# A four-layer graph kernel: each direct transfer of 125 rows issued as one of 112 and one of 13 partitions

## What is computed

```python
x = _layernorm(x + attention(x, src, dst, edge_attr_8))      # layer 0
x = _layernorm(x + message(x, src, dst, edge_type_16))       # layer 1
x = _layernorm(x + equivariant(x, src, dst, edge_attr_4))    # layer 2
x = _layernorm(x + hypergraph(x, node=src, edge=dst))        # layer 3
# each layer: x[src] gathered, work per edge, segment_sum over dst (sorted);
# layer 3: node -> edge -> node -> batch norm -> node -> edge -> node, also over sorted src
```

## Time and profile before

| | us |
|---|---|
| median of three runs | 2641.88 |
| lowest, highest | 2640.07, 2645.51 |
| the profiled execution | 2639.84 |
| its span, first to last instruction | 2638.0 |

### The profile page before, as it was taken

One profiled execution on the slowest core, in us unless ns is written; L12 is line 12 of the kernel. 1 busy time (PEld: TensorE's weight loads), 2 busy tenths in 40 slices (PEclk: granted clock), 3 DMA queues, 4 the chain that ended last, 5 costly groups with the idle time before them and its releaser, 6 DMA issues. The chain is left out here.

```text
span 2638.0 us, 21630 instructions
## 1 busy us (share of the span) xinstructions
PE 1425.5 (54%) x4580; PEld 731.6 (28%) x4580; DVE 1606.3 (61%) x4851; ACT 863.9 (33%) x1813; POOL 1861.6 (71%) x1494
## 2 busy tenths in 40 slices
PE   6787588887266666546777456444554650011211
PEld 1443244444122222212333234222222330011110
DVE  8899387788258878938777544333334554434443
ACT  0111266677235566634665511111111320000000
POOL 5773878775388886254677687777874868878787
PEclk9899799999577777768898778777777875555555
DMA  1111344443435454343454467577696873333331
GB/s 25 28 33 40 95 118 121 125 112 81 96 75 126 124 129 128 93 102 88 109 127 115 89 169 194 158 168 192 180 157 184 226 202 94 86 67 70 74 72 43
DMA packets 350927, 297.90 MB, mean 113 GB/s; under 512 B 103741, under 2 KB 305228, under 8 KB 350781
## 3 DMA queue, kind: packets, MB, share of 16 engines
q1 hardware_dynamic: 253197, 225.40, 31.1%
q0 software_dynamic: 97600, 71.11, 14.3%
HBM read 199.75 MB, written 96.70 MB: 112 GB/s over the span
## 5 line engine op out<-in xcount | busy, mean ns | idle before, releaser
L2081 PE MATMUL tl_pX<-k_ident,tl_ga 125*128 125x125 f32 x400 | 84.2, 348 | 445.7 <-DMA tl_ga<-table_TE,k_s_idxE 332.0
L2192 DVE TENSOR_TENSOR_SCAN tl_S<-tl_same,tl_S,tl_pX 128x500 f32<-128x500 bf16 x96 | 120.3, 1254 | 315.9 <-PE tl_pX L2081 178.7
L471 POOL DMA_INDIRECT tl_ga<-table_TE,k_s_idxE x200 | 244.7, 1224 | 63.4 <-issue 59.4
L2081 PEld LDWEIGHTS tl_pX<-k_ident,tl_ga 125*128 125x128 f32 x400 | 57.3, 177 | 461.9 <-DMA tl_ga<-table_TE,k_s_idxE 342.1
L471 POOL DMA_INDIRECT eq_ga<-table_T,k_idxS x100 | 124.8, 1248 | 81.9 <-ACT eq_y L1786 52.9
L471 POOL DMA_INDIRECT ms_ga<-table_T,k_idxS x100 | 132.9, 1329 | 51.6 <-issue 42.0
L471 POOL DMA_INDIRECT tl_ga<-table_TH,k_send x100 | 122.7, 1227 | 58.7 <-issue 57.8
L1261 PE MATMUL tl_pCon<-dr_BC,dn_cT 128*128 128x512 f32 x196 | 135.0, 778 | 52.9 <-ACT dn_cT L1268 29.2
L471 POOL DMA_INDIRECT at_ga<-x,k_src x100 | 131.8, 1318 | 43.4 <-issue 25.2
L273 POOL DMA_INDIRECT table_ptab<-k_ef,ix_scatI x100 | 125.1, 1251 | 45.6 <-issue 45.6
L2032 POOL DMA_INDIRECT result<-tl_o,k_dst_end x100 | 121.8, 1218 | 44.3 <-issue 29.3
(11 more groups left out here) (464 smaller groups left out, 4455.0 us busy)
## 6 DMA issues: line engine op xcount, KB each, us to landing
dr_x<-x SPq DMA_DIRECT2D x97, 256.0 KB, 7.7
result<-dr_o SPq DMA_DIRECT2D x97, 256.0 KB, 5.1
dm_xT<-xT SPq DMA_DIRECT2D x32, 768.0 KB, 6.2
table_T<-at_y SPq DMA_DIRECT2D x50, 250.0 KB
table_T<-ms_y SPq DMA_DIRECT2D x50, 250.0 KB
table_T<-eq_y SPq DMA_DIRECT2D x50, 250.0 KB
table_TE<-tl_y SPq DMA_DIRECT2D x50, 250.0 KB
tl_fac<-table_dinv SPq DMA_DIRECT2D x50, 250.0 KB, 4.7
```

What stands on the lines that cost most here:

```text
L471: nc.gpsimd.indirect_dma_start(out=buf[:, k, :], out_offset=None, in_=table, in_offset=bass.IndirectOffsetOnAxis(ap=index[:, CT * c + k:CT ...
L2081: last = nc.tensor.transpose(pX[j % 2][:, k * TP:(k + 1) * TP], ga[j % RG][:, k, :], K["ident"][0:TP, 0:TP])
L2192: nc.vector.tensor_tensor_scan(S[i][:], same[j % RM][:], pX[i][:, 0:CE], 0.0 if j % NC == 0 else S[1 - i][:, CE - 1:CE], ALU.mult, ALU.add ...
```

## The change

`copy_rows` is new. It issues a transfer of 125 partitions as two, one of partitions 0 to 111 and one of 112 to 124, on the same queue one behind the other. All 300 transfers named above go through it (225 stores, 75 loads). Each part adds 16 to the semaphore, so every wait on these semaphores asks for twice the count. Rows, tables, buffers and order are the same. The diff, with the repeated places left out:

```diff
+SPLIT = 112
...
+def copy_rows(eng, out, given, sem):
+
+
+    for part in (slice(0, SPLIT), slice(SPLIT, TP)):
+        eng.dma_start(out[part], given[part]).then_inc(sem, 16)
...
-                sp.dma_start(rows_of(T["T1"], CE * c, CT), y[c % 2][:, 0:CT, :]).then_inc(s_st[c % 2], 16)
-                sp.dma_start(rows_of(T["T1"], CE * c + E, CT), y[c % 2][:, CT:2 * CT, :]).then_inc(s_st[c % 2], 16)
+                copy_rows(sp, rows_of(T["T1"], CE * c, CT), y[c % 2][:, 0:CT, :], s_st[c % 2])
+                copy_rows(sp, rows_of(T["T1"], CE * c + E, CT), y[c % 2][:, CT:2 * CT, :], s_st[c % 2])
...
-                sp.wait_ge(s_st[i], 32 * ((NC - i + 1) // 2))
+                sp.wait_ge(s_st[i], 64 * ((NC - i + 1) // 2))
...
-                sp.dma_start(xt[c % RX][:], rows_of(T["T1"], CE * c, CT)).then_inc(s_xt[c % RX], 16)
+                copy_rows(sp, xt[c % RX][:], rows_of(T["T1"], CE * c, CT), s_xt[c % RX])
...
-                sp.dma_start(z[c % RZ][:], rows_of(T["T2"], CE * c, CT)).then_inc(s_zd[c % RZ], 16)
+                copy_rows(sp, z[c % RZ][:], rows_of(T["T2"], CE * c, CT), s_zd[c % RZ])
...
         def stored(eng, n):
-            eng.wait_ge(s_st[0], 16 * ((n + 1) // 2))
-            eng.wait_ge(s_st[1], 16 * (n // 2))
+            eng.wait_ge(s_st[0], 32 * ((n + 1) // 2))
+            eng.wait_ge(s_st[1], 32 * (n // 2))
...
-                sp.dma_start(x[e % RL][:], rows_of(T["T3"], CE * e, CT)).then_inc(s_x[e % RL], 16)
+                copy_rows(sp, x[e % RL][:], rows_of(T["T3"], CE * e, CT), s_x[e % RL])
...
-                sp.dma_start(rows_of(T[TARGET[j // NC]], CE * (j % NC), CT), y[j % 2][:]).then_inc(s_st[j % 2], 16)
+                copy_rows(sp, rows_of(T[TARGET[j // NC]], CE * (j % NC), CT), y[j % 2][:], s_st[j % 2])
```

More of the change, by code:

```diff
@@ L743, in norm @@
                 act.wait_ge(s_r, c + 1)
-                need(act, s_st[c % 2], 32 * (c // 2))
+                need(act, s_st[c % 2], 64 * (c // 2))
                 for r in range(2 * CT):
@@ L1341, in load_targets @@
                 need(sp, s_h1, c - RX + 1)
-                sp.dma_start(xt[c % RX][:], rows_of(T["T1"], CE * c, CT)).then_inc(s_xt[c % RX], 16)
+                copy_rows(sp, xt[c % RX][:], rows_of(T["T1"], CE * c, CT), s_xt[c % RX])
             def store(c):
                 sp.wait_ge(s_y, c + 1)
-                sp.dma_start(rows_of(T["T2"], CE * c, CT), y[c % 2][:, 0:CT, :]).then_inc(s_st[c % 2], 16)
-                sp.dma_start(rows_of(T["T2"], CE * c + E, CT), y[c % 2][:, CT:2 * CT, :]).then_inc(s_st[c % 2], 16)
+                copy_rows(sp, rows_of(T["T2"], CE * c, CT), y[c % 2][:, 0:CT, :], s_st[c % 2])
+                copy_rows(sp, rows_of(T["T2"], CE * c + E, CT), y[c % 2][:, CT:2 * CT, :], s_st[c % 2])
             for s in range(-4, NC + 3):
@@ L1385, in biased @@
                 have(pool, c)
-                pool.wait_ge(s_xt[c % RX], 16 * (c // RX + 1))
+                pool.wait_ge(s_xt[c % RX], 32 * (c // RX + 1))
                 need(pool, s_h2, c - RU + 1)
@@ L1540, in residual @@
                 have(dve, c)
-                dve.wait_ge(s_xt[c % RX], 16 * (c // RX + 1))
+                dve.wait_ge(s_xt[c % RX], 32 * (c // RX + 1))
                 need(dve, s_n1, c - RU + 1)
@@ L1658, in load_targets @@
                 need(sp, s_y, c - RZ + 1)
-                sp.dma_start(z[c % RZ][:], rows_of(T["T2"], CE * c, CT)).then_inc(s_zd[c % RZ], 16)
+                copy_rows(sp, z[c % RZ][:], rows_of(T["T2"], CE * c, CT), s_zd[c % RZ])
             def store(c):
                 sp.wait_ge(s_y, c + 1)
-                sp.dma_start(rows_of(T["T3"], CE * c, CT), y[c % 2][:, 0:CT, :]).then_inc(s_st[c % 2], 16)
-                sp.dma_start(rows_of(T["T3"], CE * c + E, CT), y[c % 2][:, CT:2 * CT, :]).then_inc(s_st[c % 2], 16)
+                copy_rows(sp, rows_of(T["T3"], CE * c, CT), y[c % 2][:, 0:CT, :], s_st[c % 2])
+                copy_rows(sp, rows_of(T["T3"], CE * c + E, CT), y[c % 2][:, CT:2 * CT, :], s_st[c % 2])
             for s in range(-3, NC + 4):
@@ L1782, in norm @@
                 act.wait_ge(s_r, c + 1)
-                need(act, s_st[i], 32 * (c // 2))
+                need(act, s_st[i], 64 * (c // 2))
                 for r in range(2 * CT):
@@ L1839, in residual @@
                 b = c % RZ
-                dve.wait_ge(s_zd[b], 16 * (c // RZ + 1))
+                dve.wait_ge(s_zd[b], 32 * (c // RZ + 1))
                 have(dve, c)
@@ L2133, in out @@
                 act.wait_ge(s_psR, j + 1)
-                need(act, s_st[i], 16 * (j // 2))
+                need(act, s_st[i], 32 * (j // 2))
                 if phase == 1:
@@ L2208, in added @@
                 if e < NC:
-                    dve.wait_ge(s_x[i], 16 * (e // RL + 1))
+                    dve.wait_ge(s_x[i], 32 * (e // RL + 1))
                     nc.vector.tensor_tensor(z[i][:], x[i][:], bc(b2, CT), ALU.add).then_inc(s_z, 1)
```

## The result

The changed kernel takes 2615.08 us (median of four runs, 2614.43 to 2617.21), the kernel before 2640.98 in the same comparison: a ratio of 0.9903, 95% interval 0.9885 to 0.9921, or 25.9 us less. In a later comparison it was 2615.36 against 2641.81, 0.9900 (0.9884 to 0.9915). The profiled execution took 2617.21 us, its span 2615.3, which is 22.6 us less than the profiled one of before.

What follows compares the result with a forecast made beforehand. POOL's own issuing was taken to bound most of the kernel, so only its pauses could shrink: 4.8 + 1.0 + 18 + 10 = 33.8 us off 2639.84 gives 2606, adjusted to 2608 and rounded to 2610, range 2598 to 2634.

Steps and rivals of the forecast that it cites:

- Rival A: Whole kernel: shorter landings and vanishing stalls behind 125-partition transfers give 2610 us, own range 2600 to 2622; chance 0.55.
- the crowded stretch: Second pass, 1925 to 1967 us: VectorE's two waits, 23.5 us, blamed on whole `TH` stores; 16 us counted as gain.
- rival B: Only landings get shorter; gathers slow the second pass, VectorE's waits stay with another releaser; 2629 us, chance 0.22.
- the dense load's issue: Sign in the third pass: a dense load behind a store is issued in under 1 us instead of 3.2.
- the second pause: Sign in the tail, after the third pass: POOL's wait for the last dense store about 4 us instead of 14.09.
- the first pause: Sign in the tail, before the third pass: POOL's pause about 10 us instead of 28.57.
- the waits of under 5 us near 1940: Sign in the second pass: no dense load or `TH` store is waited for over 5 us there.
- Block ends: Ends of attention, message and equivariant: last split stores land sooner, 2.4 us each for two, 1.0 for the third.
- The 28.57 us pause: POOL before the third pass: 16 us from VectorE's waits and 2.4 from the last landing, together 18.
- The 14.09 us pause: POOL after the third pass: SP stalls behind 125-partition transfers go, so 10 us (2.4 to 13.8) is gained.
- Added issues: SP's 300 extra issues, some 0.4 us each, are covered by POOL's issuing; uncovered they would cost 120 us.
- Rival C: Parts use the same paths as the whole, nothing is spread: 2640 to 2645 us, chance 0.13.

## Why the prediction was right, and where it was not

The forecast was 2610, with 2598 to 2634, and the time is 2615. Rival A's own range holds it. Its mechanism for the third pass and the block ends is the one found. For the crowded stretch rival B was nearer. That the number came out this close is in part luck: the largest term was twice what it gave, and gains in message and equivariant that the sum did not have made up for a part. Of the signs named, the dense load's issue, the two block ends and about the second pause came; the first pause, and the waits of under 5 us near 1940, did not. POOL's mean for each gather moved in attention, from 1318 to 1384 ns, which the last section takes up. The steps one by one:

**Block ends, forecast 2.4 + 2.4 + 1.0.** From first store to next load 8.0 became 5.0, 8.1 became 5.0, and 11.1 became 11.6, which gives 3.0 + 3.1 - 0.5 = 5.6 against 5.8. The third ends with POOL's scatters, as the step said. The 3.0 of attention did not reach the time: the stretch is 429.3 in both. Among the other kernels it is 424.0 to 430.7 in no order of whole or split, 466.5 with the bad cut, so the noise of this stretch is as large as the term.

**Message and equivariant, forecast nothing beyond their ends.** This step was incomplete. Message takes 450.9 to 453.2 us in the three kernels with whole transfers there and 445.0 to 448.4 in the eight whose cut is at 100 or 112 or which have three parts, 5 us less and not 3. Equivariant is 370.7 to 374.2 against 365.9 to 367.9, with the end itself no shorter. The timeline of ScalarE in the kernel before shows one reason, which I had not looked at: at its end the next rows wait for a whole store to leave their buffer.

```profile
1487.99 1.65 ACT L1786 ACTIVATE eq_y<-eq_z,eq_nb,eq_rs 125x128 f32<-125x128 f32 x4 [1.94 <-DMA table_T<-eq_y]
...
1494.00 1.65 ACT L1786 ACTIVATE eq_y<-eq_z,eq_nb,eq_rs 125x128 f32<-125x128 f32 x4 [2.06 <-DMA table_T<-eq_y]
...
1501.47 1.65 ACT L1786 ACTIVATE eq_y<-eq_z,eq_nb,eq_rs 125x128 f32<-125x128 f32 x4 [4.09 <-DMA table_T<-eq_y]
```

After the change the same instructions wait 0.47 us for VectorE.

**The 28.57 us pause, forecast 18.** It gave 7.6, and the stretch 8.6. This is the step that failed: I put the two VectorE waits down to the whole `TH` store ahead of the dense loads and counted 16 of their 23.5 us as its doing. The waits are 12.73 and 13.28 us after the change, longer if anything. What I held against rival B, that only what stands behind a `TH` store pays the second half of the delay, was a reading of two places; both lie in the one stretch where four of five rows that the gathers read are one row. Spreading that row took the waits away with whole transfers too (none over 2.9 us, and a stretch of 466.2 us), so the gathers were the cause and the whole store at most an addition. Rival B had the right culprit and no reason for it: volume, my first thought, is out, and it is where the gathers read. Its sign, another releaser for VectorE's waits, did not come either, since both still end with a dense load: what a transfer waits behind is not named as its releaser. Rival B gave this term 2.4, so the measured 7.6 lies between the two.

**The 14.09 us pause, forecast 10.** It gave 8.6, to 5.51 us (6.13 in the second profile). The step held with its mechanism: the issue of a dense load fell from 3154 to 434 ns, and the whole load put back made the next issue 5.87 us again. What remains of lag and landing is 5.5 us where I had put 4, and the first was 14.09 in this profile but 17.25 and 17.41 in two other kernels with whole transfers there; with the tail all split and no other edit it is 5.51, 6.13 and 7.63.

**Added issues, forecast no cost.** Right. A third part, 300 issues more, shows none either.

**The sum.** The profiled time fell by 22.6 us, the stretches by 22.8: 3.5 + 4.8 + 8.6 + 8.3 less the 2.4 that stand before attention, where nothing was changed (263.9 to 265.4 us in kernels with whole transfers in the layers, 265.0 to 266.5 in the others, and why I can't say). Of the 11 by which the forecast's 33.8 is too high, 9.4 are the crowded stretch (18 against 8.6).

**Rival C and the rule against splitting.** The time is 29 us below the 2644 that the rule would give. In "Rules for kernel authors" the page "DMA: Bandwidth & Descriptors" of the Trainium skill advises against two transfers to disjoint partition halves, because both halves use all 16 engines anyway. For 125 partitions the whole transfer does not (a share of 0.34 above), so cut at 112 a split pays here, and cut at 64 it is far worse than none.

## What to carry to other kernels

Look at the partition count of every direct transfer: cutting 125 into 112 and 13 gave 1%, and into 64 and 61 it cost 22%. The signs in a profile are a low share of the DMA engines while such a transfer lands alone (0.34 here), and an issue of some us right behind such a transfer, put down to whichever transfer is next in the queue; the gain here was where a chunk's transfers did not fit its time or an end waited for a landing, so compare the queue's time in a chunk with the pace of the engine that sets it. Before a slow stretch is blamed on the transfer that waits longest, look at what else fills the DMA engines and at the indices: a default row that most gathers read can cost more than any direct transfer, and a copy for each partition of a tile took that away, though in a pass without a crowd it cost 7 us.

## What was not expected of the hardware

Gathers of which 100 of 125 rows are the same 512 bytes hold up all other transfers: 141 and 144 GB/s at a DMA share of 0.89 and 0.90, against 244 GB/s at 0.83 with the row in 125 copies. They do so where four of them are issued every 6.1 us. From 1850 to 1900 us POOL issues four copies of states between every four of them, and the kernel before moves 187 GB/s at a share of 0.69:

```profile
1850.00:1900.00 50.00, 22.77 (x71) 11.97 (x69) 19.79 (x30) 6.39 (x15) 39.94 (x34) 0.76 0.69 187
```

Whether it is the row itself or the one place in memory near it, no run tells.

In the last pass the copies made it slower: POOL's scatters took 1279 and 1292 ns in the two runs with spread rows there and 1204 to 1210 in the ten other profiles. That the spread rows cause it is shown by the run that leaves them out; how, is open.

POOL's gathers of source rows in attention took 1347 to 1399 ns on average in the six profiles of kernels that split stores in layers and tail at 112 or in three parts, 1297 to 1318 in the three with whole transfers in attention, 1322 with the cut at 64 and 1283 at 100. But the kernel that splits the layers alone has 1283 too, with the same code in attention. The stretch does not follow: 426.3 us at 1399 ns, 424.0 and 430.7 at 1283 and 1393. So what sets these durations stays open.
